# Where the experts' results are stored from, and how the token table is interleaved with attention, in a two-layer fp32 kernel

## The chip, the cores and the metric

One core of one Trainium2 chip runs the whole program as one launch. The metric is the device time of the launch in microseconds. Engines are named as in the profile: PE (TensorE, matrix products and transposes), DVE (VectorE), ACT (ScalarE), POOL (GpSimd) and SP (SyncE, which only issues DMAs here; "SPq" in the rows).

## The reference

The input is x of 4 sequences x 1024 tokens x 256 channels, fp32. Layer 0 adds to x a causal attention with one head of 256 and a mixture of experts; layer 1 adds a linear attention with rotary positions and a gated feed-forward to the result. What matters for the change, cut to its core:

```python
xn = layernorm(x)
w  = softmax(causal((xn @ Wq) @ (xn @ Wk).T / 16))          # layer 0, attention
a  = w @ (xn @ Wv)
routing = softmax(xn @ Wr + br)                             # 8 experts, the best 2 of each token
gate    = the two best, normalised to sum 1
y_e = relu(xn @ W1[e] + b1[e]) @ W2[e] + b2[e]              # 256 -> 1024 -> 256
x   = x + a + sum over the token's two experts of gate * y_e
# layer 1: x = x + linear_attention(layernorm(x)) + gated_ffn(layernorm(x))
```

## The kernel before

All products are made of three products of fp32r parts (high*high, high*low, low*high): ACT makes the high part of an operand, DVE the low part, PE multiplies. There are three blocks one after the other.

**Block 1, `norm_route_attend`** (0 to 187 us in the profile). Each token is normalised, `xn` is written to DRAM as `xn_rows`, the router is computed, and each (token, expert) pair gets a row ("slot") in a table sorted by expert. Meanwhile attention runs over the first three sequences (`b` = 0, 1, 2; the fourth is done later), each in six steps `a` = 0 to 5 of one or two blocks of 128 queries. The order in a step is written by hand for each engine: PE does `scores(a + 1)`, `turn(a)`, `values(a - 1)`; DVE does `row_max(a + 1)`, `turned_lo(a)` (line 916), `add_attention(a - 1)` (line 930); ACT does `softmax(a + 1)` (line 610), `turned_hi(a)` (line 618). `turn(a + 1)` waits for `turned_lo(a)`. In step 4 PE also begins the next sequence's projection, which needs `xl`, the low part of its keys. That is made by DVE in two halves (`next_keys_lo`, line 936) from `xh`, which ACT copies in one instruction after step 1 (line 644).

The inverse table (which token lies in each of 71 blocks x 128 rows) is made in 7 groups of up to 10 slots per partition, in between the attention. For each group `find_rows` on DVE makes two 0/1 matrices, `is_block` (line 876) and `is_row` (line 878). ACT scales `is_block` with the token numbers (`scale_tokens`, line 627), PE multiplies it with `is_row` (line 480), DVE adds the result up (lines 885 and 888). The dictionary `FOUND_AFTER` names the step behind which each group is found. After the seventh group DVE writes `row_tokens` and GpSimd fetches the rows of the first tile.

**Block 2, `experts`** (187 to 655 us). The table's 9088 rows are cut into 29 tiles of 512, 256 or 128 rows, each of one expert: two big tiles (512) first, then 9 rounds of 512, 128, 256 in this order ("big", "ones", "twos" below). Tile j, of parity j % 2, needs:
- its rows: `fetch_rows` on GpSimd, one indirect DMA for each 128 rows (line 117), into the buffer of its parity. GpSimd issues those of tile j + 2 once PE has transposed the rows of tile j (`rows_turned`);
- its expert's weights: `load_weights` on SP, two DMAs of 1024 KB, W1 (line 134) and W2 (line 136), into `raw` or `raw_odd` by parity, once the weights of tile j - 2 have all been split (`w1_lo`, `w2_lo`; lines 1353 and 1363). ACT splits W1 while the tile before is computed (line 1288), DVE W2;
- its bias row `b2row` (SP, line 1145), which waits on `y_done` of an earlier tile.

PE computes a tile's hidden layer in `up` and its output in `down` (both through lines 1184 to 1186), and transposes the next tile's rows in between (`turn_rows`, line 1192), before the last `down`s of the tile. For a big tile ahead of a ones tile, the last two `down`s are done inside the ones tile (`one_block`), and with them the big tile's `add_bias` on DVE (line 1386), which writes the result tile `y` and counts `y_done`. Results are stored by GpSimd (line 1169), in the same hand-written sequence as the gathers:

```python
def fetch_and_store(tile):
    later = tile.after_next()
    if later is not None:
        hold(pool, rows_turned, tile.j + 1, passed)
        fetch_rows(pool, s, xn_rows, later)
    if not tile.is_last():
        hold(pool, y_done, tile.j + 1, passed)
        pool.dma_start(expert_out[...], y[:, tile.parity, ...]).then_inc(y_stored[tile.parity], 16)
```

The last tile is stored by SP (line 1155).

**Block 3, `combine_and_layer1`** (655 to 935 us) gathers each token's two results, adds them, does the fourth sequence's attention and layer 1. Its only contact with the change is a count: `kh_ready` continues the semaphore `xh_ready`.

Of the kernel before, what the change touches and what calls it, by code (L numbers as in the profile page):

```python
# [11 lines left out]
ALU = mybir.AluOpType  # L12
ACT = mybir.ActivationFunctionType
X = mybir.AxisListType.X
ds = bass.ds
# [124 lines left out]
def norm_route_attend(nc, s, x, Wq, Wk, Wv, Wr, br, b1, W1, W2, xn_rows):  # L140
# [3 lines left out]
    with ExitStack() as ctx:  # L144
# [116 lines left out]

            return 4 * (b - 1) + a if (b == 1 and a < 4) or (b == 2 and a < 3) else None

        FOUND_AFTER = {(0, 5): 0, (1, 0): 1, (1, 1): 2, (1, 2): 3, (1, 3): 4, (1, 5): 5, (2, 1): 6}
        assert len(GROUPS) == 7

        block = ctx.enter_context(nc.Block())
# [255 lines left out]
        def _(act):  # L523
# [81 lines left out]
            def attend(b, first, last):  # L605
                def softmax(a):
                    act.wait_ge(max_done, NS * b + a + 1)
                    for q, i, _ in rows_of(a):
                        L = (i + 1) * P
                        op = act.activation(prob[:, a % 2, 512 * q:512 * q + L], score_columns(a, q, i), ACT.Exp,  # L610
                                            bias=neg_max[:, i:i + 1], accum_out=row_sum[:, i:i + 1])
                    op.then_inc(prob_ready, 1)

                def turned_hi(a):
                    act.wait_ge(prob_turned, NS * b + a + 1)
                    act.wait_ge(attended, NS * b + a + 1)
                    n = blocks_of(a)
                    act.activation(pTh[:, a % 2, 0:n, :].rearrange("p j q -> p (j q)"),
                                   ps[:, 4:6, :].rearrange("p h k -> p (h k)")[:, 0:n * P], ACT.Copy).then_inc(pT_hi, 1)

                def scale_tokens(group):

                    act.wait_ge(block_found, group + 1)
                    columns = GROUPS[group]
                    for m in range(0, len(columns), K):
                        t = columns[m] // K
                        op = act.activation(tokens_in[:, group % 2, m:m + K, :], is_block[:, m:m + K, :],
                                            ACT.Copy, scale=token_no[:, t:t + 1])
                    op.then_inc(tokens_scaled, 1)

                if first:
                    act.wait_ge(xn_stored[1], 32)
                softmax(0)
                for a in range(NS):
                    if a + 1 < NS:
                        softmax(a + 1)
                    turned_hi(a)
                    if a == 0:
                        project_hi(b, [NPROJ - 1])
                    if (b, a) in FOUND_AFTER:  # L640
# [11 lines left out]
        def _(dve):  # L652
# [210 lines left out]
                then(V.tensor_copy(row_in_block[:, :], part_of_slot[:, :]))  # L863
                dve.wait_ge(numbers_ready, 3)

            def find_rows(group):

                columns = GROUPS[group]
                count, at, u = len(columns), slice(columns[0], columns[-1] + 1), group % 2

                def spread(a, n):
                    return a.unsqueeze(2).to_broadcast([P, count, n])

                if group > 0:
                    dve.wait_ge(tokens_scaled, group)
                V.tensor_tensor(is_block[:, 0:count, :], number[:, 0:NB].unsqueeze(1).to_broadcast([P, count, NB]),
                                spread(block_of_slot[:, at], NB), ALU.is_equal).then_inc(block_found, 1)
                V.tensor_tensor(is_row[:, u, 0:count, :], number[:, :].unsqueeze(1).to_broadcast([P, count, P]),
                                spread(row_in_block[:, at], P), ALU.is_equal).then_inc(row_found, 1)

            def sum_tokens(group, bank):

# [23 lines left out]
            def attend(b, first, last):  # L906
# [25 lines left out]
                    op.then_inc(attended, 1)  # L932

                def next_keys_lo(c):
                    dve.wait_ge(xh_ready, b + 2)
                    op = V.tensor_tensor(xl[:, (b + 1) % 2, c, :], xnT_early[:, c, (b + 1) * T:(b + 2) * T],
                                         xh[:, (b + 1) % 2, c, :].bitcast(F32), ALU.subtract)
                    if c:
                        op.then_inc(xl_ready, 1)

                row_max(0)
                for a in range(NS):
# [130 lines left out]
def experts(nc, s, W1, W2, b1, b2, W_qkv, W_r, W_k, W_v, xn_rows, expert_out):  # L1073
# [4 lines left out]
    with ExitStack() as ctx:  # L1078
# [52 lines left out]
        def _(sp):  # L1131
            def load(tile):
# [16 lines left out]
                if tile.is_last():  # L1149
                    sp.wait_ge(biased, 2 * s.COUNTS[2])  # L1150
                    for n, w in enumerate((W_r, W_k, W_v)):
                        sp.dma_start(s.wraw[:, n], w.rearrange("(c p) e -> p c e", p=P)
                                     ).then_inc(s.later_loaded, 16)
                    sp.wait_ge(y_done, MT)
                    sp.dma_start(expert_out[ds(tile.row, tile.size), :].rearrange("(s p) d -> p s d", p=P),
                                 y_rows(tile, 0, tile.parts)).then_inc(s.last_stored, 16)

            expert_tiles(sp, s, load)

        @block.gpsimd  # L1160
        def _(pool):
            def fetch_and_store(tile):
                later = tile.after_next()
                if later is not None:
                    hold(pool, rows_turned, tile.j + 1, passed)
                    fetch_rows(pool, s, xn_rows, later)
                if not tile.is_last():
                    hold(pool, y_done, tile.j + 1, passed)
                    pool.dma_start(expert_out[ds(tile.row, tile.size), :].rearrange("(s p) d -> p s d", p=P),  # L1169
                                   y[:, tile.parity, 0:tile.parts]).then_inc(y_stored[tile.parity], 16)  # L1170

            fetch_rows(pool, s, xn_rows, ExpertTile(s, None, 1))
            for lead in range(ExpertTile.LEAD):
                fetch_and_store(ExpertTile(s, None, lead))
            for n in range(3 * s.COUNTS[2]):
                fetch_and_store(ExpertTile(s, (n // 6, n % 6)))
            for u in range(2):
                pool.wait_ge(y_stored[u], 16 * (MT // 2))

        @block.tensor  # L1180
        def _(pe):
# [164 lines left out]
        def _(dve):  # L1346
# [70 lines left out]
            def body(tile):  # L1417
# [5 lines left out]
                for w in range(tile.units):  # L1423
# [8 lines left out]
                        split2(tile, w + 2)  # L1432
                    if later is None:
                        if w in (1, 2):
                            dve.wait_ge(kh_ready, s.B - 1 + w)
# [922 lines left out]
```

## Time and profile before

| | |
|---|---|
| median of 3 runs (range) | 934.88 us (931.88 to 4773.26) |
| profiled execution, its own time | 936.47 us |
| its span, first to last instruction | 934.7 us |
| PE busy | 862.1 us, 92% |
| DVE busy | 690.9 us, 74% |
| ACT busy | 524.0 us, 56% |
| POOL busy | 206.2 us, 22% |
| mean granted PE clock | 0.98 of full speed |

The profiled execution lies 1.77 us over its span and 1.6 us over the median. Busy shares are averages over three blocks with different limits. Times in the rows are microseconds from the start of the span. The granted clock is given as a share of full speed: 1.00 is 2.4 GHz, 0.50 is 1.2 GHz.

### The profile page before, as it was taken

To read this page: it belongs to the slowest core of one execution; us is meant where nothing else is said; L and a number is where in the kernel's file an instruction comes from. 1 tells how busy PE (TensorE), PEld (TensorE's weight loads), DVE (VectorE), ACT (ScalarE), POOL (GpSimd) and SP (SyncE) were. 2 spreads that over 40 slices of the span, in tenths; PEclk is the share of its full clock that TensorE was granted. 3 is DMA by queue.
4 is the path that set the end of the run, shared out by engine and by line. 5 is a ranking of instruction groups with operands and counts; after the bars stand their busy time and mean duration, and the time that the engine had idled before them with its cause. 6 is when DMAs were issued, how large, how long until landed. Compare 5 with 4: busy or idle time off the path is not lost. (4 is left out here: it accounts for less than half of the span.)

```text
span 934.7 us, 16932 instructions
## 1 busy us (share of the span) xinstructions
PE 862.1 (92%) x6067; PEld 769.6 (82%) x6067; DVE 690.9 (74%) x1306; ACT 524.0 (56%) x944; POOL 206.2 (22%) x215
## 2 busy tenths in 40 slices
PE   4998979889989898989998989699989999999998
PEld 3787969879979898988888888699878787978877
DVE  6788656566777868777777868567487989899874
ACT  5633444265556555646464646454458867686781
POOL 1000000130131313131213130310703527154202
PEclk9999989999999999999999999799999999999999
DMA  9302000083456565565747474632401212021101
GB/s 292 104 1 90 1 1 1 24 270 134 147 189 203 189 199 190 197 215 172 252 135 253 151 252 164 224 119 63 102 18 29 64 45 73 19 84 51 45 1 46
DMA packets 70770, 112.40 MB, mean 120 GB/s; under 512 B 7552, under 2 KB 55360, under 8 KB 70720
## 3 DMA queue, kind: packets, MB, share of 16 engines
q1 hardware_dynamic: 61584, 84.99, 27.4%
q0 software_dynamic: 9136, 26.75, 9.4%
q8 instruction: 31, 0.51, 0.2%
q14 instruction: 19, 0.16, 0.1%
HBM read 94.02 MB, written 17.69 MB: 120 GB/s over the span
## 5 line engine op out<-in xcount | busy, mean ns | idle before, releaser
L1322 ACT ACTIVATE h<-ps,b1T 128x512 f32<-128x512 f32 (+1 forms) x160 | 90.6, 589 | 150.6 <-PE ps L1186 148.0
L1184 PE MATMUL ps<-w2h,hh 128*128 128x256 f32 x568 | 165.1, 291 | 0.0
L1185 PE MATMUL ps<-w2l,hh 128*128 128x256 f32 x568 | 163.0, 287 | 0.0
L1186 PE MATMUL ps<-w2h,hl 128*128 128x256 f32 x568 | 162.8, 287 | 0.0
L1427 DVE TENSOR_TENSOR hl<-h,hh 128x512 fp32r<-128x512 f32 x124 | 85.5, 690 | 65.6 <-ACT hh L1326 59.6
L1184 PEld LDWEIGHTS ps<-w2h,hh 128*128 128x128 f32 x568 | 111.0, 195 | 2.5 <-DVE hl L1427 0.2
L1185 PEld LDWEIGHTS ps<-w2l,hh 128*128 128x128 f32 x568 | 111.1, 196 | 2.0
L1184 PE MATMUL ps<-xTh,w1h 128*128 128x512 f32 (+1 forms) x320 | 110.6, 346 | 2.4 <-DVE xTl L1369 2.4
L1186 PEld LDWEIGHTS ps<-w2h,hl 128*128 128x128 f32 x568 | 111.1, 196 | 0.0
L1185 PE MATMUL ps<-xTl,w1h 128*128 128x512 f32 (+1 forms) x320 | 110.6, 346 | 0.0
L1186 PE MATMUL ps<-xTh,w1l 128*128 128x512 f32 (+1 forms) x320 | 109.9, 344 | 0.0
L1169 POOL DMA_DIRECT2D expert_out<-y x28 | 20.3, 726 | 337.9 <-DVE y L1386 337.8
L117 POOL DMA_INDIRECT rows<-xn_rows,row_tokens x49 | 55.3, 1129 | 174.0 <-DVE row_tokens L893 154.3
L1326 ACT ACTIVATE hh<-h 128x512 fp32r<-128x512 f32 x124 | 78.4, 632 | 3.9
L127 POOL DMA_INDIRECT raw<-expert_out,slots x48 | 59.0, 1229 | 61.3 <-PE ps L1704 49.1
L1184 PEld LDWEIGHTS ps<-xTh,w1h 128*128 128x128 f32 x320 | 61.3, 192 | 8.0 <-DVE xTl L1369 2.6
L1186 PEld LDWEIGHTS ps<-xTh,w1l 128*128 128x128 f32 x320 | 61.1, 191 | 7.4
L1185 PEld LDWEIGHTS ps<-xTl,w1h 128*128 128x128 f32 x320 | 61.2, 191 | 5.0
L1702 PE MATMUL ps<-wqkvh,xh 128*128 128x256 f32 (+1 forms) x128 | 43.7, 341 | 2.4 <-DVE folded L2079 2.4
L1386 DVE TENSOR_TENSOR y<-ps,b2row 128x512 f32<-128x512 f32 (+1 forms) x39 | 23.5, 625 | 27.7 <-PE ps L1186 27.2
L610 ACT ACTIVATE shared<-ps,neg_max 128x1024 f32<-128x1024 f32 (+7 forms) x24 | 17.7, 739 | 46.4 <-DVE neg_max L910 46.4
L1363 DVE TENSOR_TENSOR w2l<-raw,w2h 128x512 fp32r<-128x512 f32 x60 | 41.8, 697 | 2.1
(328 smaller groups left out, 2246.6 us busy)
## 6 DMA issues: line engine op xcount, KB each, us to landing
raw<-in_L_ffn_W SPq DMA_DIRECT2D x30, 1024.0 KB, 6.8
raw_odd<-in_L_ffn_W SPq DMA_DIRECT2D x28, 1024.0 KB
expert_out<-y POOLq DMA_DIRECT2D x11, 512.0 KB
shared<-in_L_ffn_b SPq DMA_DIRECT2D x9, 512.0 KB
b2row<-in_L_ffn_b SPq DMA_DIRECT2D x29, 128.0 KB, 7.3
x_acc<-in_L_attn_x SPq DMA_DIRECT2D x3, 1024.0 KB, 9.1
xn_rows<-raw SPq DMA_DIRECT2D x3, 1024.0 KB, 4.4
out<-x_acc SPq DMA_DIRECT2D x3, 1024.0 KB
```

The costliest lines, as they stand in the source:

```text
L117: pool.indirect_dma_start(out=rows_part(s, tile, part), out_offset=None, in_=xn_rows, in_offset=bass.IndirectOffsetOnAxis(ap=token, axis=0 ...
L127: pool.indirect_dma_start(out=s.picked_rows[:, i, k, :], out_offset=None, in_=expert_out, in_offset=bass.IndirectOffsetOnAxis(ap=slot, axi ...
L1169: pool.dma_start(expert_out[ds(tile.row, tile.size), :].rearrange("(s p) d -> p s d", p=P), y[:, tile.parity, 0:tile.parts]).then_inc(y_st ...
L1184: pe.matmul(out, ah, bh, start=start, stop=False, skip_group_check=True)
L1185: pe.matmul(out, ah, bl, start=False, stop=False, skip_group_check=True)
L1186: return pe.matmul(out, al, bh, start=False, stop=stop, skip_group_check=True)
L1322: op = act.activation(h32[:, at, cols], ps[:, slot, cols], ACT.Relu, bias=s.b1T[:, ds(e * HC + w * tile.chunks + n, 1)])
L1326: act.activation(hh[:, slot, 0:tile.width], h32[:, at, 0:tile.width], ACT.Copy).then_inc(h_hi, 1)
L1363: V.tensor_tensor(w2l[:, u, ks], w2raw[u][:, ks], w2h[:, u, ks].bitcast(F32), ALU.subtract).then_inc(w2_lo, 1)
L1386: op = V.tensor_tensor(y_rows(tile, half, n), ps[:, bank:bank + n, half // 2 * D:(half // 2 + 1) * D], b2row[:, tile.b2_slot, :].unsqueeze ...
L1427: V.tensor_tensor(hl[:, slot, at], h32[:, slot % 2, at], hh[:, slot, at].bitcast(F32), ALU.subtract).then_inc(h_lo, 1)
L1702: pe.matmul(dst, ah(c), bh(c), start=(c == 0), stop=False)
```

## The change

Four edits.
1. GpSimd only fetches rows in `experts`. The stores of tiles 0 to 27 move to SP, where the store of tile j - 2 is issued behind the loads for tile j. The two last ones follow at the end. SP's hardware loop over the tiles is written out.
2. In block 1 `find_rows` is cut in two: `find_blocks` (`is_block`) stays where the group was found (group 5 one step earlier), `find_rows` (`is_row`) moves to one place ahead of `turned_lo` in the step after.
3. ACT's copy `xh` of 128 x 2048 is cut into two of 128 x 1024, after steps 1 and 2.
4. Counts on `xh_ready` follow from that (in block 3 too).

```diff
-        FOUND_AFTER = {(0, 5): 0, (1, 0): 1, (1, 1): 2, (1, 2): 3, (1, 3): 4, (1, 5): 5, (2, 1): 6}
+        BLOCKS_AFTER = {(0, 5): 0, (1, 0): 1, (1, 1): 2, (1, 2): 3, (1, 3): 4, (1, 4): 5, (2, 1): 6}
+        ROWS_AHEAD = {(1, 0): 0, (1, 1): 1, (1, 2): 2, (1, 3): 3, (1, 4): 4, (1, 5): 5, (2, 2): 6}
...
                     turned_hi(a)
                     if a == 0:
                         project_hi(b, [NPROJ - 1])
-                    if (b, a) in FOUND_AFTER:
-                        scale_tokens(FOUND_AFTER[b, a])
-                    if a == 1 and not last:
-
-                        act.activation(xh[:, (b + 1) % 2], xnT_early[:, :, (b + 1) * T:(b + 2) * T], ACT.Copy
+                    if (b, a) in BLOCKS_AFTER:
+                        scale_tokens(BLOCKS_AFTER[b, a])
+                    if a in (1, 2) and not last:
+                        act.activation(xh[:, (b + 1) % 2, a - 1], xnT_early[:, a - 1, (b + 1) * T:(b + 2) * T], ACT.Copy
                                        ).then_inc(xh_ready, 1)
...
-            def find_rows(group):
+            def find_blocks(group):
+
+                count, at = columns_of(group)
                 if group > 0:
                     dve.wait_ge(tokens_scaled, group)
                 V.tensor_tensor(is_block[:, 0:count, :], ...).then_inc(block_found, 1)
-                V.tensor_tensor(is_row[:, u, 0:count, :], ...).then_inc(row_found, 1)
+
+            def find_rows(group):
+
+                count, at = columns_of(group)
+                V.tensor_tensor(is_row[:, group % 2, 0:count, :], ...).then_inc(row_found, 1)
...
+                    if (b, a) in ROWS_AHEAD:
+                        find_rows(ROWS_AHEAD[b, a])
                     turned_lo(a)
...
-                    if (b, a) in FOUND_AFTER:
-                        find_rows(FOUND_AFTER[b, a])
+                    if (b, a) in BLOCKS_AFTER:
+                        find_blocks(BLOCKS_AFTER[b, a])
...
-            expert_tiles(sp, s, load)
+
+            def store(tile):
+                sp.wait_ge(y_done, tile.j + 1)
+                done = s.last_stored if tile.is_last() else y_stored[tile.parity]
+                sp.dma_start(expert_out[ds(tile.row, tile.size), :].rearrange("(s p) d -> p s d", p=P),
+                             y_rows(tile, 0, tile.parts)).then_inc(done, 16)
+
+            tiles = [ExpertTile(s, None, lead) for lead in range(ExpertTile.LEAD)]
+            tiles += [ExpertTile(s, (n // 6, n % 6)) for n in range(3 * s.COUNTS[2])]
+            for n, tile in enumerate(tiles):
+                load(tile)
+                if n > 1:
+                    store(tiles[n - 2])
+            for tile in tiles[-2:]:
+                store(tile)
...
-            def fetch_and_store(tile):
+            def fetch(tile):
                 later = tile.after_next()
                 if later is not None:
                     hold(pool, rows_turned, tile.j + 1, passed)
                     fetch_rows(pool, s, xn_rows, later)
-                if not tile.is_last():
-                    hold(pool, y_done, tile.j + 1, passed)
-                    pool.dma_start(expert_out[ds(tile.row, tile.size), :].rearrange("(s p) d -> p s d", p=P),
-                                   y[:, tile.parity, 0:tile.parts]).then_inc(y_stored[tile.parity], 16)
```

## Rows read from the trace of the kernel before

**Rows 1.** The waits of PE in the whole span: total us, times, longest.
```profile
PE ps L1192 <- DMA shared<-xn_rows,row_tokens: 25.0, 8, 7.6
PE ps L470 <- DVE pTl L916: 7.6, 6, 2.2
PE ps L412 <- DVE xl L936: 4.1, 2, 3.2
```

**Rows 2.** Timeline of PE, one round and 602 us: start, duration, [idle before <- releaser].
```profile
438.87 0.38 PE L1192 MATMUL ps<-ident,rows 128*128 128x128 f32 x2
...
446.98 0.65 PE L1241 MATMUL ps<-ident,h 128*128 128x128 f32 x4 [0.24 <-DVE h L1396]
...
460.22 0.44 PE L1192 MATMUL ps<-ident,rows 128*128 128x128 f32 x2 [2.09 <-DMA shared<-xn_rows,row_tokens]
...
602.11 0.69 PE L1192 MATMUL ps<-ident,rows 128*128 128x128 f32 x2 [7.61 <-DMA shared<-xn_rows,row_tokens]
```

**Rows 3.** Timeline of POOL: big's store, last gather of next big, and at 595.
```profile
451.59 0.82 POOL L1169 DMA_DIRECT2D expert_out<-y  x1 [24.48 <-DVE y L1386]
...
456.51 0.95 POOL L117 DMA_INDIRECT shared<-xn_rows,row_tokens  x1 [0.30 <-issue]
...
595.35 1.36 POOL L117 DMA_INDIRECT shared<-xn_rows,row_tokens  x1 [0.30 <-issue]
```

**Rows 4.** Windows behind two of the waits for rows and behind the `xl` wait.
```profile
core 0: us, PE busy (x) PEld busy (x) DVE busy (x) ACT busy (x) POOL busy (x), PEclk, DMA share, GB/s
132.00:136.00 4.00, 3.89 (x18) 2.98 (x19) 1.75 (x5) 1.72 (x5) 0.00 (x0) 0.50 0.00 0
326.00:328.00 2.00, 2.00 (x11) 2.00 (x11) 2.00 (x3) 0.95 (x2) 0.00 (x0) 0.50 1.05 373
604.00:606.00 2.00, 2.00 (x11) 2.00 (x10) 0.83 (x1) 1.88 (x3) 0.00 (x0) 0.50 0.85 330
```

**Rows 5.** Timeline of SP: first tiles' issues, then W1 for the next big.
```profile
187.90 0.35 SPq L1145 DMA_DIRECT2D b2row<-in_L_ffn_b  x1
189.02 0.37 SPq L134 DMA_DIRECT2D raw_odd<-in_L_ffn_W  x1
...
443.46 0.37 SPq L134 DMA_DIRECT2D raw_odd<-in_L_ffn_W  x1
```

**Rows 6.** Landing of one W1 and W2 pair: issued at 432, and at 368 us.
```profile
DMA to landing us min/median/max: 4.9/6.3/7.7
DMA to landing us min/median/max: 6.3/8.2/10.1
```

**Rows 7.** Timeline of DVE in two rounds: big's result, a cast, rows' low part.
```profile
449.72 1.29 DVE L1386 TENSOR_TENSOR y<-ps,b2row 128x512 f32<-128x512 f32 x2
...
451.98 0.66 DVE L1361 CAST w2h<-raw 128x512 fp32r<-128x512 f32 x1
...
508.94 1.23 DVE L1369 TENSOR_TENSOR xTl<-ps,xTh 128x1024 fp32r<-128x1024 f32 x1 [1.23 <-ACT xTh L1292]
```

**Rows 8.** Timeline of ACT: first use of next big tile's W1, two rounds.
```profile
456.81 0.61 ACT L1288 ACTIVATE w1h<-raw_odd 128x512 fp32r<-128x512 f32 x1
...
503.08 0.61 ACT L1288 ACTIVATE w1h<-raw 128x512 fp32r<-128x512 f32 x1
...
506.36 0.63 ACT L1326 ACTIVATE hh<-h 128x512 fp32r<-128x512 f32 x1
507.89 1.02 ACT L1292 ACTIVATE xTh<-ps 128x1024 fp32r<-128x1024 f32 x1 [0.89 <-PE ps L1192]
```

**Rows 9.** Timeline of DVE in attention, sequence 1, steps 2 and 3.
```profile
121.96 1.48 DVE L878 TENSOR_TENSOR is_row<-number,row_in_block 128x1280 f16<-128x1280 f16 x1
...
127.16 0.82 DVE L916 TENSOR_TENSOR pTl<-ps,pTh 128x640 fp32r<-128x640 f32 x1 [1.79 <-ACT pTh L618]
```

**Rows 10.** Timeline of ACT there: the copy of the next sequence's keys.
```profile
116.16 1.90 ACT L644 ACTIVATE xh<-xnT_early 128x2048 fp32r<-128x2048 f32 x1
```

**Rows 11.** Timeline of PE there: the projection waiting for the low keys.
```profile
132.11 0.80 PE L412 MATMUL ps<-xh,folded 128*128 128x512 f32 x1 [3.24 <-DVE xl L936]
```

More of the change, by code:

```diff
@@ L864, in parts_of_slots, with columns_of @@
                 dve.wait_ge(numbers_ready, 3)
-            def find_rows(group):
+            def columns_of(group):
                 columns = GROUPS[group]
-                count, at, u = len(columns), slice(columns[0], columns[-1] + 1), group % 2
-                def spread(a, n):
-                    return a.unsqueeze(2).to_broadcast([P, count, n])
+                return len(columns), slice(columns[0], columns[-1] + 1)
+            def find_blocks(group):
+                count, at = columns_of(group)
                 if group > 0:
@@ L876, in find_rows @@
                 V.tensor_tensor(is_block[:, 0:count, :], number[:, 0:NB].unsqueeze(1).to_broadcast([P, count, NB]),
-                                spread(block_of_slot[:, at], NB), ALU.is_equal).then_inc(block_found, 1)
-                V.tensor_tensor(is_row[:, u, 0:count, :], number[:, :].unsqueeze(1).to_broadcast([P, count, P]),
-                                spread(row_in_block[:, at], P), ALU.is_equal).then_inc(row_found, 1)
+                                block_of_slot[:, at].unsqueeze(2).to_broadcast([P, count, NB]), ALU.is_equal
+                                ).then_inc(block_found, 1)
+            def find_rows(group):
+                count, at = columns_of(group)
+                V.tensor_tensor(is_row[:, group % 2, 0:count, :], number[:, :].unsqueeze(1).to_broadcast([P, count, P]),
+                                row_in_block[:, at].unsqueeze(2).to_broadcast([P, count, P]), ALU.is_equal
+                                ).then_inc(row_found, 1)
             def sum_tokens(group, bank):
@@ L934, in next_keys_lo @@
                 def next_keys_lo(c):
-                    dve.wait_ge(xh_ready, b + 2)
+                    dve.wait_ge(xh_ready, 2 * b + c + 2)
                     op = V.tensor_tensor(xl[:, (b + 1) % 2, c, :], xnT_early[:, c, (b + 1) * T:(b + 2) * T],
@@ L1153, in load @@
                                      ).then_inc(s.later_loaded, 16)
-                    sp.wait_ge(y_done, MT)
-                    sp.dma_start(expert_out[ds(tile.row, tile.size), :].rearrange("(s p) d -> p s d", p=P),
-                                 y_rows(tile, 0, tile.parts)).then_inc(s.last_stored, 16)
-            expert_tiles(sp, s, load)
+            def store(tile):
[11 more added lines that the diff above has]
+                store(tile)
+            for u in range(2):
+                sp.wait_ge(y_stored[u], 16 * (MT // 2))
         @block.gpsimd
         def _(pool):
-            def fetch_and_store(tile):
+            def fetch(tile):
                 later = tile.after_next()
@@ L1166, in fetch_and_store @@
                     fetch_rows(pool, s, xn_rows, later)
-                if not tile.is_last():
-                    hold(pool, y_done, tile.j + 1, passed)
-                    pool.dma_start(expert_out[ds(tile.row, tile.size), :].rearrange("(s p) d -> p s d", p=P),
-                                   y[:, tile.parity, 0:tile.parts]).then_inc(y_stored[tile.parity], 16)
             fetch_rows(pool, s, xn_rows, ExpertTile(s, None, 1))
             for lead in range(ExpertTile.LEAD):
-                fetch_and_store(ExpertTile(s, None, lead))
+                fetch(ExpertTile(s, None, lead))
             for n in range(3 * s.COUNTS[2]):
-                fetch_and_store(ExpertTile(s, (n // 6, n % 6)))
-            for u in range(2):
-                pool.wait_ge(y_stored[u], 16 * (MT // 2))
+                fetch(ExpertTile(s, (n // 6, n % 6)))
         @block.tensor
@@ L1434, in body @@
                         if w in (1, 2):
-                            dve.wait_ge(kh_ready, s.B - 1 + w)
+                            dve.wait_ge(kh_ready, 2 * s.B - 3 + w)
                             V.tensor_tensor(kl[:, :, key_half(w - 1)], s.xnT_last[:, :, key_half(w - 1)],
```

## The prediction, made before the changed kernel was run

> **What bounds the kernel now.** I read the page first: PE is busy 92% of the span, so the question is what fills its idle time and whether the change touches that. The view of waits, for PE alone, answers it [rows 1]: the longest entry is not an engine but a DMA, 25.0 us in 8 waits before line 1192, the transposes of a tile's gathered rows. There are 8 rounds in which a big tile follows a twos tile, and the timeline of PE shows one such wait in each, always ahead of the big tile's rows (3.53, 2.35, 2.41, 2.34, 2.09, 2.35, 2.32 and 7.61 us) [rows 2]. The timeline of POOL says why [rows 3]. Of the four gathers of the next big tile the last is issued at 456.51 us, but the buffer has been free since the ones tile's rows were turned at 438.87 [rows 2]. GpSimd stood 24.48 us in front of the store of the big tile's result, and the gathers stand behind that store. PE is through with `up` of the twos tile at 458.1 (460.22 - 2.09), when the last of them has not landed.
>
> The wait costs more than its length. In some rounds the granted clock falls to 0.5, the 1.2 GHz level, after PE has idled: 0.50 at 326 to 328 us and at 604 to 606 [rows 4], while the rounds of 278, 370, 415, 506 and 551 us stay at 1.00. The matmul starts lie 0.21 us apart there instead of 0.12. I count 3.4, 3.4 and 6.0 us of busy PE time at the low level behind the waits of 324, 460 and 602 us. Half of that is lost: 1.7 + 1.7 + 3.0 = 6.4 us. The distances between the big tiles' transposes agree: 45.0 us in four undipped rounds, 46.6 and 46.5 with a dip.
>
> In block 1 PE waits 7.6 us for DVE's `pTl` and 4.1 us for `xl` [rows 1], nearly all of it in sequences 0 and 1, where DVE and ACT carry the table work.
>
> **Part 1, gathers alone on GpSimd.** A fetch now waits only for `rows_turned`. For the big tile that is 438.87 + 0.4 = 439.3 us. Four gathers at the present spacing of 1.26 us end by 444.5, 13 us before PE asks. Even in the slowest case the rows are there 5.4 us after the end of the last issue (595.35 + 1.36 against 602.11) [rows 2, 3]. So all eight waits go, 25.0 us, and with them the clock loss of 6.4 us: 31.4 us.
>
> What the moved gathers meet: DVE. One cast of 0.42 us took 0.66 us while GpSimd wrote descriptors [rows 7]. In the new place, 439 to 444.5, one or two such casts run ahead of the ones block, where DVE is already 0.24 us late for PE [rows 2]. I charge 0.1 us a round, 1 us in all. The two ends are 0 and 8 x 0.5 = 4 us.
>
> **Part 2, the stores on SP.** The order on SP is now loads of tile j, store of tile j - 2, loads of tile j + 1. The store waits for `y_done` of tile j - 2, and behind it on SP's queue stand the value load of the expert's number, W1, W2 and the bias row of tile j + 1. For most tiles this changes nothing, since the loads are released later than the store anyway. The exception is the big tile after a ones tile. Its W1 and W2 go out at 443.46 us now, when the ones tile's weights have been split [rows 5]. Afterwards they stand behind the store of the previous big tile, whose `y` is finished at 449.72 + 1.29 = 451.0 [rows 7]. Nobody else waits for SP at that moment. The step that decides is thus the landing of this W1, 8 times:
> - GpSimd's store starts 0.6 us after that end (451.59 [rows 3]); SP may react as late or faster, I take 0.2 to 0.6, so the store is issued at 451.2 to 451.6;
> - the store's issue takes some 0.4 us, value load plus issue gap 0.77 us (from 188.25 to 189.02 [rows 5]): W1 at 452.4 to 452.8;
> - alone on the queues W1 lands 4.9 us after issue, and W2 2.7 us later; in the busiest window it is 6.3 [rows 6]. The store's 512 KB ahead of it, at the 330 to 373 GB/s of the stretches in [rows 4], take 1.4 to 1.6 us, but its issue is 1.2 us earlier, so little is left to wait for: I take 0 to 1.3 us. W1 lands between 457.3 and 460, likeliest 458.3.
>
> ACT wants it at 456.81 [rows 8]. It will therefore stand, and the question is how long PE is covered. From the round at 503: the first split starts at 503.08 = S, the last `hh` of the twos tile ends at S + 3.9 (506.99) [rows 8], and without the wait for rows `xTh` would end at S + 4.9 and `xTl` at S + 6.2 (1.02 and 1.23 us [rows 7, 8]). Without its stall PE has `up` done at 458.0, 0.85 us of transposes, then four `down`s of 1.45 us, until 464.7. It needs `hl` of the third unit at 461.75 (S + 2.7, so S up to 459.0), that of the fourth at 463.2 (S + 4.6, so 458.6), and `xTl` at 464.7 (458.5). So PE loses about S - 458.5 a round: 0 for a landing at 458.3, up to 1.7 us for 460 (S follows the landing by 0.2). I charge 0.3 us x 8 = 2.4 us. The bounds are 0 and 14.
>
> The loads have lost their slack: 443.46 + 4.9 = 448.4 was 8.4 us ahead of use. The other items moved with them are covered. W2 (461) is first used in the big tile at 472. The bias row waited for `y_done` of the ones tile before and still does. The ones' store now stands behind the 2 MB of this load, but the next writer of that `y` half comes tens of microseconds later. The written-out loop on SP costs SP instructions but no engine waits on it elsewhere. At the end of the block the last store leaves at the same `y_done` as before.
>
> The wait on the DMA queue deserves a second look. As the Trainium skill has it (DMA: Bandwidth & Descriptors, "Queues, rings and completion order"), SP owns one row of rings and descriptors in a ring are consumed in order, while different rows are served in turn. By that rule W1 stands fully behind the 512 KB store now that both are on SP's row, where GpSimd's store shared the engines with it. By the page's rate of 436 GB/s this would be an estimated 1.2 us, which lies inside the bounds that the rows gave; no row of the kernel before shows a store and a load on SP's queue together.
>
> **Part 3, the table in block 1.** DVE's step in sequence 1 is a closed loop: `is_block`, `is_row` (1.48 us [rows 9]), row maximum, ACT's softmax and `turned_hi`, DVE's `turned_lo`, with DVE idle 1.79 us ahead of the latter [rows 9]. Moved ahead of `turned_lo`, `is_row` fits into that idle time, as gaps of 2.08, 1.87, 2.83, 1.79 and 1.79 us stand there in the five steps. Redoing the steps by hand: step 2's softmax can't begin at once, because ACT still copies `xh` until 118.0 [rows 10]; halved, the copy ends near 117.2 and `turned_lo(2)` comes 0.8 us earlier. Steps 3 and 4 gain another 0.7 and 1.3 us. The low keys, on which PE stands until 132.11 [rows 11], are ready at 129.1 + 0.2 instead of 132.0. From there PE has its own work until the sequence ends, so the gain is 2.8 us. It may be 2.5 more if the low clock behind that wait (0.50 from 132 to 136) is gone; PE would still idle about 1.5 and 2.2 us there, so I don't count it. In sequence 0 DVE is held by the routing arithmetic, in sequence 2 PE has no such wait: nothing. Group 5 comes one step earlier, ahead of ACT's `turned_hi(5)`, which falls 0.9 + 1.6 us later; over four microseconds of the next sequence's projection on PE cover this. Lower end of part 3: 0, if a moved instruction only trades places; upper 5.3.
>
> **Sum.** -31.4 + 1 + 2.4 - 2.8 = -30.8 us against the profiled execution's 936.5: 905.7, and 1.6 us less against the median. I write 905.
>
> **Rivals.**
> 1. W1 lands later than the cover. For: its slack of 8.4 us is spent, and landings of 6.3 us have occurred with other traffic about [rows 6]. At 460.2 the loss is 8 x 1.9 = 15 us, 12 to 13 more than I charged (917 us); at 461 it is 20 us plus clock dips in some rounds, since waits of 2.1 to 2.35 us brought one in two rounds of seven [rows 2, 4]: 925 to 930. Against: in the new place the gathers are gone from the queues and only the store is there.
> 2. The same mechanism past the break-even, slower than before. If SP's row drains the store, W1 and W2 so that ACT can start only at 463 or later, PE waits 4.6 us or more a round, plus 1.7 us of clock: 8 x 6.3 = 50 us against 34 gained, 950 us. It decides at a landing near 461.5 to 462.5, that is 9.5 us after issue for the first megabyte, against 4.9 to 6.3 seen. Unlikely.
> 3. The gathers come early but PE meets another wait at once (weights' splits, `hl`), so that the removed 25 us return. PE waits on nothing else in those rounds above 0.25 us [rows 2], and behind the wait ACT and DVE still idle 0.89 and 1.23 us [rows 7, 8]; half the gain lost would give 920.
> 4. The change doesn't do what it says: GpSimd reaches the gathers no earlier because the twos' fetch ahead of it is late. That fetch is released by the previous big transposes, 20 us before, so hardly: 932.
>
> **How the numbers follow.** Forecast (landing at or before 459.3, 896 to 913 us): 0.62. Rival 1: 0.2, of which a third ends below 916. Rival 3: 0.1, a third of it below 916. Rival 2: 0.04. Rival 4 and the rest: 0.04. A change of 2% (18.7 us, to 916.2 or 953.6) is about what a measurement of this kernel can tell from none. Faster by over 2%: 0.62 + 0.07 + 0.03 = 0.72; slower by over 2%: 0.03; within: 0.25. The range runs from 896 (all bounds good: -31.4 - 5.3 and the median's 1.6, with a little more clock) to 926 (most of rival 1).
>
> **What would show it.** Right: no wait of PE on gathered rows; the four gathers at the ones' transposes, GpSimd's waits on `rows_turned` alone; W1 of the big tile issued 1.2 to 1.5 us after `y_done`, ACT standing 1 to 2 us before line 1288; rounds of 42.7 to 44.5 us; `xl` in sequence 1 near 129. Wrong: rounds of 45 us or more, or ACT standing over 3 us on W1 and PE behind it, or the clock below 0.98.

## The result: 902.0 us, 0.967 of the time before

| | before | changed |
|---|---|---|
| median | 933.38 us (lowest 931.12) | 901.98 us (899.21 to 902.68) |
| ratio | | 0.9666, 95% interval 0.9629 to 0.9702 |
| profiled execution | 936.5 us, span 934.7 | 899.21 us, span 897.5 |
| PE busy, granted clock | 92% | 95%, 0.994 |

The spans differ by 37.2 us, the medians by 31.4. The profiled execution of before was 3.1 us above its median and that of the changed kernel 2.8 us below its own; that makes up the 5.9 us. One of the four executions of the kernel before took 4773.26 us; the median of the other three is 931.88, and the ratio is taken without it.

Read the waits of PE in the changed kernel first, against [rows 1]:

```profile
engine line waited for: us in total, times, longest us
PE ps L342 <- DMA b1r<-in_L_ffn_b: 7.3, 1, 7.3
PE ps L471 <- DVE pTl L922: 5.4, 6, 1.9
...
PE ps L413 <- DVE xl L942: 2.7, 2, 1.8
...
PE ps L1255 <- DVE h L1410: 2.6, 9, 0.3
```

The 25.0 us before the transposes of gathered rows are gone as an entry; PE waits for rows in no round. No other entry has taken their place: the only one that repeats from round to round in the expert block is 0.3 us in each of nine rounds. The timeline of PE gives the length of a round; these are the ones tile's rows being turned, its hidden rows, and the next big tile's rows being turned with no idle time ahead of them (compare [rows 2]):

```profile
420.50 0.38 PE L1206 MATMUL ps<-ident,rows 128*128 128x128 f32 x2
...
428.68 0.43 PE L1255 MATMUL ps<-ident,h 128*128 128x128 f32 x2 [0.31 <-DVE h L1410]
...
439.68 0.38 PE L1206 MATMUL ps<-ident,rows 128*128 128x128 f32 x2
```

The L1255 waits stand at 258.48, 301.02, 343.57, 386.13, 428.68, 471.23, 513.78, 556.32 and 598.74 us: 42.55 us a round, where it was 45.0, or 46.5 with a dip of the clock. GpSimd now issues the four gathers right at the ones' transposes, held by `rows_turned` alone (compare [rows 3]):

```profile
421.67 0.94 POOL L117 DMA_INDIRECT rows<-xn_rows,row_tokens  x1 [20.15 <-PE ps L1206]
...
425.42 0.95 POOL L117 DMA_INDIRECT shared<-xn_rows,row_tokens  x1 [0.30 <-issue]
```

The last is issued by 426.4, and the rows are turned at 439.68: 13 us in hand. The same round on DVE (`y` of big), SP (the store, then the next big tile's W1, W2 and bias row) and ACT (first use of that W1), to set beside [rows 5, 7, 8]:

```profile
431.42 1.29 DVE L1400 TENSOR_TENSOR y<-ps,b2row 128x512 f32<-128x512 f32 x2
432.63 0.42 DVE L1375 CAST w2h<-raw 128x512 fp32r<-128x512 f32 x1
...
432.74 0.37 SPq L1166 DMA_DIRECT2D expert_out<-y  x1
433.91 0.38 SPq L134 DMA_DIRECT2D raw_odd<-in_L_ffn_W  x1
434.38 0.45 SPq L136 DMA_DIRECT2D raw_odd<-in_L_ffn_W  x1
435.33 0.34 SPq L1153 DMA_DIRECT2D b2row<-in_L_ffn_b  x1
...
438.96 0.63 ACT L1302 ACTIVATE w1h<-raw_odd 128x512 fp32r<-128x512 f32 x1 [0.35 <-DMA raw_odd<-in_L_ffn_W]
```

`y_done` comes at 431.42 + 1.29 = 432.71; SP issues the store at once (432.74), W1 1.2 us after `y_done`, and ACT begins to split it at 438.96, after standing 0.35 us. From issue to first use are 5.05 us, from `y_done` 6.25. This is the earliest of the eight rounds: over all of them ACT stands 0.28 to 1.21 us, the first use comes 5.05 to 5.90 us after the issue (5.45 on average) and 6.25 to 7.10 us after `y_done`. PE has no wait behind it in any of them. The cast of 0.66 us [rows 7] takes 0.42 again.

In block 1, PE's wait for the low keys of the next sequence ends 4.93 us earlier than in [rows 11], and the low clock behind it is shorter: in the windows of two microseconds it is back at 1.00 in the third, where [rows 4] has 0.50 from 132 to 136.

```profile
127.18 0.50 PE L413 MATMUL ps<-xh,folded 128*128 128x512 f32 x1 [1.84 <-DVE xl L942]
```
```profile
core 0: us, PE busy (x) PEld busy (x) DVE busy (x) ACT busy (x) POOL busy (x), PEclk, DMA share, GB/s
128.00:130.00 2.00, 2.00 (x15) 1.39 (x14) 1.61 (x2) 1.68 (x5) 0.00 (x0) 0.52 0.00 0
130.00:132.00 2.00, 2.00 (x13) 2.00 (x13) 0.61 (x2) 0.00 (x0) 0.00 (x0) 0.63 0.00 0
132.00:134.00 2.00, 2.00 (x15) 1.82 (x15) 1.31 (x3) 0.00 (x0) 0.00 (x0) 1.00 0.00 0
```

To compare kernels I cut the span at two instructions of PE: the first transposes of gathered rows after the table (187.23 us before, 181.60 now), where the expert stage starts, and the first transposes of the next layer's attention (655.00 before, 617.59 now), where it ends.

So block 1 is 5.6 us shorter, the expert stage 467.8 - 436.0 = 31.8 us shorter, and the rest is the same within 0.2 us (279.7 and 279.9).

### The profile page after: what moved, and what is told of

It is laid out like the page before. It is cut to its first block and busy times, and to the rows that moved or that the text cites. A ratio compares the mean times of both kernels' runs of the same rounds, so it can differ in the third digit from the quotient of the medians.

```text
span 897.5 us, 16848 instructions
## 1 busy us (share of the span) xinstructions
PE 852.9 (95%) x6067; PEld 762.8 (85%) x6067; DVE 689.2 (77%) x1306; ACT 523.8 (58%) x946; POOL 173.2 (19%) x187
## 5 line engine op out<-in xcount | busy, mean ns | idle before, releaser
L1198 PE MATMUL ps<-w2h,hh 128*128 128x256 f32 x568 | 162.8, 287 | 0.0
L1200 PE MATMUL ps<-w2h,hl 128*128 128x256 f32 x568 | 160.7, 283 | 0.0
L1199 PE MATMUL ps<-w2l,hh 128*128 128x256 f32 x568 | 160.6, 283 | 0.0
L117 POOL DMA_INDIRECT rows<-xn_rows,row_tokens x49 | 49.4, 1007 | 471.1 <-PE ps L1206 310.8
L1198 PEld LDWEIGHTS ps<-w2h,hh 128*128 128x128 f32 x568 | 108.6, 191 | 2.4 <-DVE hl L1441 0.2
L1199 PEld LDWEIGHTS ps<-w2l,hh 128*128 128x128 f32 x568 | 108.7, 191 | 2.1
L1200 PEld LDWEIGHTS ps<-w2h,hl 128*128 128x128 f32 x568 | 108.6, 191 | 0.0
L1717 PE MATMUL ps<-wqkvl,xh 128*128 128x256 f32 (+1 forms) x128 | 43.3, 338 | 0.0
L1718 PE MATMUL ps<-wqkvh,folded 128*128 128x256 f32 (+1 forms) x128 | 43.1, 337 | 0.0
```

Source lines behind the costliest of these rows:

```text
L117: pool.indirect_dma_start(out=rows_part(s, tile, part), out_offset=None, in_=xn_rows, in_offset=bass.IndirectOffsetOnAxis(ap=token, axis=0 ...
L1198: pe.matmul(out, ah, bh, start=start, stop=False, skip_group_check=True)
L1199: pe.matmul(out, ah, bl, start=False, stop=False, skip_group_check=True)
L1200: return pe.matmul(out, al, bh, start=False, stop=stop, skip_group_check=True)
L1717: pe.matmul(dst, ah(c), bl(c), start=False, stop=False)
L1718: mm = pe.matmul(dst, al(c), bh(c), start=False, stop=(c == DC - 1))
```

## The experiments

The experiments ran on three chips: the four kernels from "stores only" to "weights first" on the first, the next four on the second, the last two on the third. The kernel before had a median of 926.57 us on the first (923.6 to 931.0), 926.77 on the second (922.5 to 935.4) and 939.60 on the third (938.2 to 941.2), so I compare the experiments by the lengths of their stages, and by the ratio where the question is the gain. The changed kernel itself ran only on the second of them. "xl" is where PE's wait for the low keys ends.

| kernel | median us | ratio (95%) | stage starts | length of expert stage | xl |
|---|---|---|---|---|---|
| before (first profile) | 933.38 | 1 | 187.23 | 467.8 | 132.11 |
| changed (first profile) | 901.98 | 0.9666 (0.9629 to 0.9702) | 181.60 | 436.0 | 127.18 |
| stores only | 904.52 | 0.9750 (0.9715 to 0.9784) | 188.39 | 436.7 | 132.80 |
| table only | 923.97 | 0.9977 (0.9951 to 1.0002) | 179.96 | 460.2 | 127.06 |
| GpSimd reordered | 903.77 | 0.9755 (0.9719 to 0.9792) | 186.18 | 436.0 | 131.17 |
| weights first | 902.02 | 0.9731 (0.9697 to 0.9764) | 183.03 | 437.6 | 127.50 |
| changed, again | 901.06 | 0.9707 (0.9642 to 0.9772) | 182.71 | 436.3 | 127.36 |
| weights 2 us later | 904.20 | 0.9729 (0.9661 to 0.9797) | 183.19 | 439.5 | 128.78 |
| weights 4 us later | 931.36 | 1.0030 (0.9995 to 1.0066) | 182.87 | 467.2 | 128.52 |
| bias first | 895.99 | 0.9647 (0.9583 to 0.9712) | 182.90 | 433.0 | 127.44 |
| copy whole | 900.46 | 0.9579 (0.9559 to 0.9599) | 181.86 | 436.8 | 127.46 |
| rows together | 904.73 | 0.9631 (0.9607 to 0.9656) | 185.61 | 436.2 | 131.29 |

### The two halves of the change apart

**Stores only.** Block 1 of the kernel before, with the changed code of SP and GpSimd (the last two hunks of the diff above).

> Block 1 as before, stores on SP and gathers alone on GpSimd as in the change. Theory A (the waits of PE on gathered rows, 25.0 us, and the clock loss behind them, 6.4 us, were the store's place ahead of the gathers): about 30 us below the kernel before, ratio 0.966 to 0.972, no wait of PE on gathered rows, block 2 some 436 us long as in the changed kernel, and no more than 6 us slower than the changed kernel. Rival B (a good part of the gain came from block 1): 15 to 20 us below before.

Measured: 904.52 us, the stage at 436.7, no wait of PE for rows. The expert stage is as short as in the changed kernel, and xl stays where it was. But the time is only 22 us below the kernel before, between theory A's 30 and rival B's 15 to 20, and the ratio misses the expected 0.966 to 0.972. The lengths decide for theory A: the stage has all of its shortening. The likely reason for the ratio is a shorter wait for rows in the kernel before on this chip, as the next kernel shows.

**Table only.** The changed block 1, with the loops of SP and GpSimd of before.

> Block 1 as in the change, block 2 as before. Theory A: 3 to 6 us below the kernel before (2.8 us of waiting and up to 2.5 us of clock), ratio 0.993 to 0.997; eight waits of PE on gathered rows of some 25 us in all stay. Rival B: 15 us below before.

Measured: 923.97 us, 2.6 us less than before, a little under the 3 to 6 expected, and with an interval that just includes 1, so the time alone doesn't show this gain. The two gains add up, though: "weights first", which has both halves and, as shown below, gains nothing from its own edit, is 24.6 us below before on this chip, 2.5 of them more than "stores only". xl comes as early as in the changed kernel. The waits for rows are back (line 1200 turns the rows here):

```profile
PE ps L1200 <- DMA shared<-xn_rows,row_tokens: 17.9, 8, 7.4
```

They sum to 17.9 us instead of 25.0 [rows 1]: 1.77, 1.06, 1.10, 2.42, 1.86, 1.07, 1.19 and 7.40 us. The stage is 460.2 long, 7.6 less than in the first profile of before. The same expert code thus waited 7.1 us less here. A kernel with such waits can differ from chip to chip where the changed one doesn't; but its executions also differ by 13 us on one chip (922.5 to 935.4), and nothing here separates the chip from what varies between executions.

### Is it the engine, or the order?

**GpSimd reordered.** The kernel before, with the stores left on GpSimd, but each behind the fetch of the next tile:

```diff
-            def fetch_and_store(tile):
+            def fetch(tile):
...
+            for n, tile in enumerate(tiles):
+                fetch(tile)
+                if n > 0:
+                    store(tiles[n - 1])
```

> The kernel before, with one edit: GpSimd still stores, but the store of a tile stands behind the gathers that the next tile releases. Theory A (only the order on GpSimd's queue counted): as fast as the kernel with stores on SP and block 1 as before, within 2 us, ratio to before 0.966 to 0.972. Rival C (GpSimd's store issues cost something themselves, by slowing VectorE's casts or by late gathers): 5 us or more slower than that kernel.

Measured: 903.77 us and a stage of 436.0, the same as "stores only" within their spread, as theory A had it; its ratio of 0.9755 misses the expected one for the same reason as that of "stores only". The timeline of its GpSimd shows what changed: the big tile's gathers no longer stand behind its store, which now follows them.

```profile
426.34 0.97 POOL L117 DMA_INDIRECT rows<-xn_rows,row_tokens  x1 [15.69 <-PE ps L1195]
...
430.13 0.95 POOL L117 DMA_INDIRECT shared<-xn_rows,row_tokens  x1 [0.31 <-issue]
437.99 0.82 POOL L1170 DMA_DIRECT2D expert_out<-y  x1 [6.92 <-DVE y L1389]
```

So what gains is that the gathers pass the store. Which queue carries the store is worth nothing that shows here.

### What the weights' place behind the store costs

**Weights first.** The changed kernel, with the store of tile j - 3 behind the loads of tile j, so that no weights stand behind a store that is due:

```diff
-                if n > 1:
-                    store(tiles[n - 2])
-            for tile in tiles[-2:]:
+                if n > 2:
+                    store(tiles[n - 3])
+            for tile in tiles[-3:]:
```

> The changed kernel, with each store one tile later on SP, behind the loads of the third next tile instead of the second. W1 of the big tile leaves at once again, some 8 us earlier. Theory A (PE is covered against W1's landing): ScalarE's wait on the weights, some 0.35 us a round, goes, the time stays within 1 us of the changed kernel. Rival D (W1's lateness costs PE something hidden): 2 to 5 us below the changed kernel.

Measured: 902.02 us, stage 437.6. W1 leaves at 428.05 us here, 7.5 us ahead of the big tile's `y_done`, and ACT never stands on it. The changed kernel did not run on this chip, so I compare rounds: seven of the eight take 42.55 us on average, as there; the other one has a second wait for `h`, of 0.62 us, and is 0.8 us longer. Since W1 without the store ahead of it gives no shorter round, its place behind the store costs PE nothing. **Changed, again** ran on the second chip as the mark for the next three:

> The changed kernel itself once more, as the mark for the runs beside it. Theory A: 899 to 903 us, or lower by what this chip's kernel before is lower; rounds of 42.5 us in block 2.

It took 901.06 us, the stage 436.3. Its first split comes 6.37 to 7.13 us after `y_done`.

**Weights 2 us later** and **weights 4 us later** measure how much cover is left. SP waits for one thing more before the weights of a big tile:

```diff
                         sp.wait_ge(w2_lo, NQ * (tile.j - 1))
+                        if tile.kind == 0 and tile.j > 2:
+                            sp.wait_ge(y_done, tile.j - 1)    # 2 us; for 4 us: sp.wait_ge(h_lo, tile.unit - 3)
```

> The changed kernel, but SP holds the weights of a big tile until the ones tile's result is finished too, some 1.7 us later. Theory A (PE is covered until the first split of W1 starts 7.5 us after the big tile's result is finished, and it starts at 6.2 us now): ScalarE stands about 2 us on the weights in each of 8 rounds, PE loses 0.3 to 0.6 us a round, 2 to 5 us in all. Rival D (no cover left now): 1.7 us a round and more, 14 us or more.

> The changed kernel, but SP holds the weights of a big tile until VectorE has the first low part of the hidden layer of the twos tile, some 4.2 us later than now. Theory A: first split 10.4 us after the big tile's result, 2.9 us past the cover, so PE waits about 2.9 us in 8 rounds, 23 us, plus clock loss in some rounds (up to 1.7 us each): 923 to 935 us, as slow as the kernel before. Rival E (the cover is larger, because the order of ScalarE's work absorbs it): under 12 us lost.

Measured for the first: 904.20 us, stage +3.2 us, rounds of 42.7 to 43.3 us, in the 2 to 5 us of theory A. (W1 was issued 1.5 us later, not quite 2.) For the second: 931.36 us, stage 467.2, +30.9 us, in the forecast 923 to 935 as well: the whole gain of the change is gone. Its waits of PE, its SP, the first split on ACT and PE's wait in one round:

```profile
PE ps L1200 <- DVE hl L1443: 19.2, 11, 2.4
```
```profile
314.74 0.38 SPq L134 DMA_DIRECT2D raw<-in_L_ffn_W  x1
...
318.65 5.81 SPq L1151 DMA_DIRECT2D shared<-in_L_ffn_b  x1
```
```profile
319.81 0.63 ACT L1304 ACTIVATE w1h<-raw 128x512 fp32r<-128x512 f32 x1 [4.58 <-DMA raw<-in_L_ffn_W]
```
```profile
322.61 0.39 PE L1200 MATMUL ps<-w2h,hh 128*128 128x256 f32 x1 [2.40 <-DVE hl L1443]
```
```profile
core 0: us, PE busy (x) PEld busy (x) DVE busy (x) ACT busy (x) POOL busy (x), PEclk, DMA share, GB/s
321.00:323.00 2.00, 0.39 (x3) 0.39 (x4) 1.30 (x3) 1.97 (x5) 0.00 (x0) 0.97 0.74 249
323.00:325.00 2.00, 2.00 (x11) 2.00 (x11) 1.17 (x3) 1.97 (x4) 0.00 (x0) 0.50 0.97 377
325.00:327.00 2.00, 2.00 (x14) 2.00 (x14) 2.00 (x3) 0.69 (x2) 0.00 (x0) 0.68 1.01 404
327.00:329.00 2.00, 2.00 (x12) 1.67 (x11) 0.80 (x2) 0.16 (x1) 0.00 (x0) 1.00 1.09 351
```

Read them as a chain. ACT stands 4.58 us for W1 where it stood 0.3 to 1.2, its splits delay the `hh` of the twos tile, DVE's `hl` follows, and PE waits 2.2 to 2.4 us in eight rounds. Behind the wait the clock is at 0.50 and then 0.68 for four microseconds; five of the eight rounds have such a dip. Of the 30.9 us, 19.2 are waits for `hl`. Cut into nine stretches of 47 us from 190 us on, the stage has a mean granted clock of 0.96 in five and 1.00 in four: 5 x 0.04 x 47 = about 9.4 us lost to it. That leaves some 2 us which I can't place.

The length of a round, from one big tile's `y_done` to the next, says how much cover PE has. It holds more than the one wait that the list shows:

| kernel | first split of W1 after `y_done` | round longer than in "changed, again" |
|---|---|---|
| changed, again | 6.37 to 7.13 us | |
| weights 2 us later | 7.52 to 8.06 us | 0.15 to 0.67 us |
| weights 4 us later, the first and the seventh round (no dip) | 10.28 and 10.29 us | 2.88 and 3.02 us |

Both delays fit one rule: PE loses what the first split comes later than 7.4 us after `y_done`. (The single rounds give 7.3 to 7.5.) So the changed kernel has only 0.3 to 1.1 us of cover left. In "weights 4 us later" the rounds with a dip are 4.1 to 4.4 us longer; one without a dip is 4.0 longer, which this rule doesn't explain.

### A version that beats both

**Bias first.** The only wait that all rounds of the changed kernel share is the 0.3 us before the ones tile's hidden rows (L1255). DVE adds the bias to the second half after one more piece of the next tile's W1. I exchanged them:

```diff
                 bias_rows(tile, 0)
-                split1(later, 3)
                 bias_rows(tile, 1)
+                split1(later, 3)
```

> The changed kernel, with VectorE's second bias_rows ahead of the last split of W1 in the ones block. It aims at the only wait of PE left in a round, 0.3 us in 9 ones blocks. Theory A: that wait goes, nothing else comes late, 2 to 3 us below the changed kernel. Rival F: the low part of the hidden layer is late next, no gain.

Measured: 895.99 us, 5.1 less than the changed kernel on the same chip, more than the 2 to 3 expected; the stage is 3.3 us shorter. The L1255 entry is gone from its waits. On DVE the second addition now starts 0.16 us behind PE's result, and the split comes after it:

```profile
426.43 0.68 DVE L1410 TENSOR_TENSOR h<-ps,shared 128x512 f32<-128x512 f32 x1
427.27 0.69 DVE L1410 TENSOR_TENSOR h<-ps,shared 128x512 f32<-128x512 f32 x1 [0.16 <-PE ps L1200]
427.87 0.68 DVE L1367 TENSOR_TENSOR w1l<-raw,w1h 128x512 fp32r<-128x512 f32 x1
```

The waits were 2.9 us in the changed kernel on this chip, most of the stage's 3.3. The spans of the two profiled executions differ by 3.4 us (899.0 and 895.6), so nothing of size changed elsewhere; the medians differ by more because the profiled execution of this one was the slowest of its four. The gain lies between 3 and 5 us.

### The two parts of block 1

**Copy whole.** The changed kernel with `xh` copied by one instruction again, after step 1:

```diff
-                    if a in (1, 2) and not last:
-                        act.activation(xh[:, (b + 1) % 2, a - 1], xnT_early[:, a - 1, (b + 1) * T:(b + 2) * T], ACT.Copy
-                                       ).then_inc(xh_ready, 1)
+                    if a == 1 and not last:
+                        act.activation(xh[:, (b + 1) % 2], xnT_early[:, :, (b + 1) * T:(b + 2) * T], ACT.Copy
+                                       ).then_inc(xh_ready, 2)
```

> The changed kernel with ScalarE's copy of the next sequence's keys in one instruction again (after step 1). Theory A: softmax(3) in sequence 1 starts 0.9 us later and the later steps keep that, so the low keys are ready 0.9 us later; time 0 to 2 us above the changed kernel.

**Rows together.** The changed kernel with `is_row` behind `is_block` again, and so behind `turned_lo`:

```diff
-                    if (b, a) in ROWS_AHEAD:
-                        find_rows(ROWS_AHEAD[b, a])
                     turned_lo(a)
...
                         find_blocks(BLOCKS_AFTER[b, a])
+                        find_rows(BLOCKS_AFTER[b, a])
```

> The changed kernel with is_row made right behind is_block again, at the changed places. Theory A (is_row was in VectorE's closed loop): of the 3.9 us by which the low keys of sequence 1 came earlier, 2.5 to 3.5 us are lost again; time 3 to 6 us above the changed kernel. Rival G (the halved copy did most of it): under 1.5 us lost.

To take out what happens earlier, I count from the first row maximum of step 1 in sequence 1 (at 102.03 before, 100.99 in the changed kernel). From there to the end of PE's wait for the low keys: 30.08 us before, 26.19 changed, 26.54 with the copy whole, 29.25 with the rows together. The split of the copy is worth 0.35 us, not the 0.9 expected, although it brings the next step's `turned_lo` 0.87 us forward; the order of `is_row` is worth 3.06 us, as theory A had it. In the times the first doesn't show (900.46 us, the changed kernel 901.98 and 901.06 on other chips); "rows together" is 4.3 us above "copy whole" on the same chip. With it the gap on DVE is back (rows together, timeline of DVE, then of PE):

```profile
126.34 0.82 DVE L922 TENSOR_TENSOR pTl<-ps,pTh 128x640 fp32r<-128x640 f32 x1 [1.79 <-ACT pTh L619]
...
127.81 0.89 DVE L876 TENSOR_TENSOR shared<-number,block_of_slot 128x710 f16<-128x710 f16 x1
128.61 1.49 DVE L883 TENSOR_TENSOR is_row<-number,row_in_block 128x1280 f16<-128x1280 f16 x1
130.01 1.22 DVE L942 TENSOR_TENSOR xl<-xnT_early,xh 128x1024 fp32r<-128x1024 f32 x1
```
```profile
131.29 0.79 PE L413 MATMUL ps<-xh,folded 128*128 128x512 f32 x1 [2.92 <-DVE xl L942]
```

In the changed kernel `is_row` stands ahead of that `pTl`, DVE idles 0.91 us there instead of 1.79, and nothing but `is_block` lies between it and the low keys (compare [rows 9]):

```profile
121.24 1.48 DVE L883 TENSOR_TENSOR is_row<-number,row_in_block 128x1280 f16<-128x1280 f16 x1
123.64 0.82 DVE L922 TENSOR_TENSOR pTl<-ps,pTh 128x640 fp32r<-128x640 f32 x1 [0.91 <-ACT pTh L619]
...
125.10 0.89 DVE L876 TENSOR_TENSOR shared<-number,block_of_slot 128x710 f16<-128x710 f16 x1
125.91 1.22 DVE L942 TENSOR_TENSOR xl<-xnT_early,xh 128x1024 fp32r<-128x1024 f32 x1
```

## Why the prediction was right, and where its terms were off

The forecast was 905.0 us, the median is 901.98. The steps in their order:

**Part 1, the waits and their clock: right.** I had 25.0 + 6.4 = 31.4 us. The eight waits are gone, the granted clock is 1.00 in the windows of the stage from 192 us on, and the stage is 31.8 us shorter. Both halves show apart: "stores only" has it without the table, "table only" does not. That the same expert code on another chip waits 17.9 us, not 25.0, was not in the prediction: the term is what this one profile shows. The ratio of the changed kernel is 0.967 and 0.971 in its two measurements.

**The charge of 1 us for gathers beside DVE: about half of it came.** PE's wait for `h` grew from 0.24 to 0.30 us, 0.06 x 9 = 0.5 us. It goes with the gathers' place: 2.1 us in all where they stand behind the store (before, "table only"), 2.6 and 2.8 where they don't ("stores only", "GpSimd reordered").

**Part 2, the landing of W1: right in mechanism, the charge of 2.4 us too high.** I put W1's issue at 1.4 to 1.8 us after `y_done`; it was 1.2, as SP reacts at once (0.03 us) where I took 0.2 to 0.6. I took 0 to 1.3 us for waiting behind the store. The trace has the landing of this W1 in four of the eight rounds: 5.1, 5.3, 5.5 and 5.8 us after the issue, where the one alone took 4.9 [rows 6], so 0.2 to 0.9 us of it came; the split follows the landing at once. It started 6.25 to 7.10 us after `y_done`, where I had 7.5 as the point from which PE loses: the term is 0, not 2.4, and "weights first" confirms that there is nothing to gain. "Weights 4 us later" shows the same: with the store some 5.5 us ahead W1 is in use 4.98 us after its issue on average, with the store 1.2 us ahead 5.45 us. By the rule of the Trainium skill (DMA: Bandwidth & Descriptors, "Queues, rings and completion order"), W1 stands behind the 512 KB in SP's ring, by an estimate from that page's rate for 1.2 us from the store's issue on. The rows don't decide on the rule: W1 was issued 1.17 us after the store (432.74 and 433.91), so the store could have been through by then, and the half microsecond can be a rest of it or other traffic. No run here issues the two without that distance.

**The cover of 7.5 us: right, and nearly spent.** Late weights put numbers to rival 1. The two delays give 7.4 us (the table above), so the step-by-step reading of ACT's and DVE's work behind `y_done` holds to 0.1 us. In the round shown, `y` was finished at 309.16 and the split began 10.65 us later; my rule gives 3.15 us, the wait of PE alone is 2.40, the two undipped rounds are 2.9 and 3.0 us longer. The same experiment bears out rival 1 as a mechanism: 4.2 us of delay cost 30.9 us. It did not happen because the landing was early, not because PE was safe from it: in the latest round 0.3 us more, in the earliest 1.1, would have begun to cost. Rival 2 is the same mechanism further on, at a delay that no run here has. ([Rows 6] puts W2 some 3.3 us behind W1, not 2.7 as I had it; nothing rested on that.)

**Part 3: the right gain from the right place, too small.** I had 2.8 us with bounds of 0 and 5.3. Counted from the row maximum it is 3.9 us. (In the medians of one chip, "stores only" against "weights first", block 1's change shows as 2.5 us.) The working by steps holds up: from that anchor the `pTl` of step 1 comes 0.75 us earlier, that of step 2 another 0.86, of step 3 0.87, and the low keys 1.41, where I had 0, 0.8, 0.7 and 1.3. The term that I missed is the first: `is_row` had also stood ahead of the row maximum of step 2. The split of the copy, to which I gave the 0.8 us of step 2, does bring that `pTl` 0.87 us forward, but only 0.35 of it reaches the low keys. The remaining difference of block 1 is about 1 us of clock at 78 to 86 us, 0.50 to 1.00 in single windows before and 1.00 in the changed kernel; in the second profile of the changed kernel it is low again there (0.55 and 0.60 from 78 to 82 us), so it is not the change's.

**Of the signs** that I named, three missed narrowly on the good side: rounds of 42.5 us, not 42.7 to 44.5; ACT standing 0.3 to 1.2 us on W1, not 1 to 2; and `xl` at 127.2, not near 129.

**Rival 3** (another wait at once) fell: the list of waits has none. **Rival 4** fell: GpSimd reached the gathers at the ones' transposes.

**The sum.** By the two profiles: -31.8 in the stage, -5.6 in block 1, +0.2 in the rest, 37.2 us, against 30.8 predicted. Of the 6.4 us, 3.8 are the stage (the 2.4 for W1, 0.5 for DVE, 0.9 in nothing that I can name), 1.1 the low keys, about 1.5 clock and rest in block 1. My own sum gave 904.1 for the median (905.7 less 1.6), and I wrote 905. That it lies within 3 us of 901.98 is partly luck: the profiled execution of before, 936.5 us, was slower than the 931 to 935 of the others and that of the changed kernel the fastest of its four, so the terms are off by 6.4 us where the medians are off by 3.

## What to carry over

When PE waits for a prefetch, look first at what stands ahead of it in its own queue and was released later: here moving four gathers past one store took 2.5% off the time ("GpSimd reordered"), and the engine that carried the store made no difference. Before loading a queue anew, work out from the consumer's chain how late its transfers may land, and then measure it by delaying them: 1.5 us more cost 3 us, and 4.2 us cost all of the gain. If a step is bound to finish last on one engine, put its filler into the gap in which that engine waits for another (3.1 us by `is_row` alone), and look at the short wait that repeats in every round: 0.3 us x 9 gave 3 to 5 us in the best version.

## What the runs showed of the hardware

- The kernel that waits for transfers differed between four measurements (933.4, 926.6, 926.8 and 939.6 us), and by 13 us within one of them; the changed one, whose transfers have cover, hardly did (902.0 and 901.1, all executions within 899.2 to 902.7).
- A 1 MB load that was issued 1.17 us behind a 512 KB store on the same queue was in use 5.05 to 5.90 us after its issue (5.45 on average of eight); with the store some 5.5 us ahead it took 4.87 to 5.07 (4.98).
- With more transfers queued, SP's issue of a 512 KB load took 5.81 us instead of 0.44 (5.1 to 5.8 us in six of eight rounds), and the bias row behind it on SP was issued only at 324.64 us (weights 4 us later, the first rows above).
- Waits of 2.2 to 2.4 us on PE were followed by a clock of 0.5 for two to four microseconds in five of eight rounds of "weights 4 us later"; those of 0.3 us never were in the changed kernel. In block 1 a wait of 1.84 us was followed by 0.52 and 0.63 as well.
